# A two-layer convolution kernel on one core: every SBUF region that TensorE reads starts at one phase modulo 1024 bytes

## What is computed

```python
# layer 0: bottleneck with a deformable 3x3 convolution
out = relu(bn(conv1x1(x, w1)))                 # 1024 -> 256 channels
offset = conv3x3(out, w_off, b_off)            # 18 offsets per pixel
out = relu(bn(deform_conv3x3(out, offset, w2)))  # bilinear samples at 9 shifted places, 256 -> 256
x1 = relu(bn(conv1x1(out, w3)) + x)            # 256 -> 1024 channels
# layer 1: a kernel attention block
t, p, g = Wt @ x1, Wp @ x1, Wg @ x1            # 1024 -> 512 channels each
att[k] = sum(a_k * p**k * g);  y = sum_k a_k * att[k] * t**k    # k = 0, 1, 2, sums over a whole image
z = Wz @ y                                     # 512 -> 1024 channels
out = (z - mean) * rsqrt(var + eps) * gn_w + gn_b + x1          # mean, var over a whole image
```

## The kernel before

| tiles | stage, part in the matmul | before | after |
|---|---|---|---|
| `xh`, `xl`, `w1h`, `w1l`, `w2h`, `w2l` | 1, both operands | 544 (32) | 160 (32) |
| `o1h0`, `o1l0` / `o1h1`, `o1l1` | 1, both | 544 / 32 (32) | 160 / 672 (32) |
| `x1h`, `x1l` | 2, moving | 544 (32) | 160 (32) |
| `wlh0` to `wlh10`, `wll0` to `wll10`, `w3h`, `w3l` | 2, weights | 544 (32) | 160 (32) |
| `wlh11`, `wll11` | 2, weights of group 11 | 672 (32) | 160 (32) |
| `ao`, `acl`, `ident` | 2, transposes | 128, 544, 448 (0, 32, 64) | 160 (32) |
| `yh`, `yl`, `wzh` | 3, moving, weights | 544 (32) | 160 (32) |
| `wzl` | 3, weights of L196 | 128 (0) | 160 (32) |
| `g0_0` to `g1_2`, `xs`, `xb`, `tb` | not read by TensorE | 128 (0) | 160 (32) |
| `z44` to `z47`, `z70`, `stage`, `g1_3` | not read by TensorE | 672 (32) | 160 (32) |
| the other `z` tiles but `z69` | not read by TensorE | 544 (32) | 160 (32) |

## Time and profile before

### The profile page before, as it was taken

The page is one execution under the profiler, slowest core; times in us unless marked ns, Lnnn a source line. Parts: engine busy times, 40 slices in busy tenths (PEclk is TensorE's granted clock), DMA queues, the critical chain, the costliest instruction groups (busy, mean ns, idle before and its releaser), DMA issues.

```text
span 2339.6 us, 29804 instructions
## 1 busy us (share of the span) xinstructions
PE 2236.2 (96%) x10252; PEld 1853.8 (79%) x10252; DVE 1573.2 (67%) x3177; ACT 1252.9 (54%) x2432; POOL 794.7 (34%) x706
## 2 busy tenths in 40 slices
PE   8999999999989999999999999999999999999970
PEld 6888888888868888888888888888888878887750
DVE  4222324766788898889888988898884334467855
ACT  6444545453455565556555655565563324456745
POOL 0100003434224665566566766676651000000000
PEclk9999999999999999999999999999999999999985
DMA  9998889999998998898889889998883111118869
GB/s 304 313 314 287 303 299 376 399 401 393 403 374 290 315 333 312 305 327 315 304 308 326 307 305 312 318 322 307 310 319 128 72 54 36 54 52 295 313 229 388
DMA packets 289824, 667.97 MB, mean 286 GB/s; under 512 B 27112, under 2 KB 101608, under 8 KB 283528
## 3 DMA queue, kind: packets, MB, share of 16 engines
q0 software_dynamic: 88048, 322.81, 39.3%
q1 hardware_dynamic: 172536, 262.59, 31.5%
q10 hardware_dynamic: 29088, 80.67, 9.3%
HBM read 435.47 MB, written 230.49 MB: 285 GB/s over the span
## 4 chain that ended last, share of the span: by engine, by line
PE 87%; DVE 5%; DMA 4%; SPq 2%; ACT 1%; issue 1%; POOL 0%; ACTq 0%; DVEq 0%
PE bank L194 23%; PE bank L196 23%; PE bank L195 23%; PE bank L1458 5%; PE bank L1459 5%; PE bank L1460 5%; DVE z L1402 2%; PE bank L1476 2%; DMA xs<-x 1%; DMA g<-vwide,tbl 1%; SPq L458 1%; SPq L462 1%; PE bank L1500 0%; PE bank L1484 0%; DMA xt<-x 0%
## 5 line engine op out<-in xcount | busy, mean ns | idle before, releaser
L643 POOL DMA_INDIRECT g<-vwide,tbl x512 | 605.4, 1182 | 509.9 <-DVE a L1030 214.4
L194 PE MATMUL bank<-x1h,wlh 128*128 128x512 f32 x1536 | 603.1, 393 | 3.5 <-DVE x1l L1292 3.5
L196 PE MATMUL bank<-x1h,wll 128*128 128x512 f32 x1536 | 600.1, 391 | 0.0
L195 PE MATMUL bank<-x1l,wlh 128*128 128x512 f32 x1536 | 599.3, 390 | 0.0
L1030 DVE SCALAR_TENSOR_TENSOR a<-g,tbl,a 128x256 f32<-128x256 f32 x1224 | 529.0, 479 | 25.0 <-DMA g<-vwide,tbl 18.0
L670 ACT ACTIVATE g<-g,tbl 128x256 f32<-128x256 f32 x1008 | 427.1, 499 | 217.9 <-DMA g<-vwide,tbl 179.3
L194 PEld LDWEIGHTS bank<-x1h,wlh 128*128 128x128 f32 x1536 | 288.8, 188 | 64.0 <-issue 3.7
L196 PEld LDWEIGHTS bank<-x1h,wll 128*128 128x128 f32 x1536 | 288.6, 188 | 62.2
L195 PEld LDWEIGHTS bank<-x1l,wlh 128*128 128x128 f32 x1536 | 289.0, 188 | 60.7
L748 ACT ACTIVATE vb<-bank 128x512 f32<-128x512 f32 (+1 forms) x320 | 174.2, 554 | 191.1 <-PE bank L1460 161.4
L1458 PE MATMUL bank<-w2h,o1h 128*128 128x512 f32 (+1 forms) x640 | 236.7, 370 | 0.0
(11 more groups left out here) (154 smaller groups left out, 3206.6 us busy)
## 6 DMA issues: line engine op xcount, KB each, us to landing
vwide<-vb SPq DMA_DIRECT2D x256, 256.0 KB, 5.8
vwide<-vb SPq DMA_DIRECT2D x112, 512.0 KB, 5.3
xf<-in_x SPq DMA_DIRECT2D x32, 1024.0 KB, 6.4
x<-xf ACTq DMA_DIRECT2D x32, 1024.0 KB, 7.0
out<-z SPq DMA_DIRECT2D x128, 256.0 KB, 5.1
xin<-in_x ACTq DMA_DIRECT2D x54, 512.0 KB, 5.5
t<-ts ACTq DMA_DIRECT2D x64, 256.0 KB, 5.0
tb<-t POOLq DMA_DIRECT2D x16, 1024.0 KB, 5.8
```

The source lines that it names most:

```text
L194: nc.tensor.matmul(out, wh, xh, start=first, stop=False)
L195: nc.tensor.matmul(out, wh, xl, start=False, stop=False)
L196: return nc.tensor.matmul(out, wl, xh, start=False, stop=last)
L643: pool.indirect_dma_start(slot[:].rearrange("p a c -> p (a c)"), None, d["vwide"][img], bass.IndirectOffsetOnAxis(ap=at[:, i, tap(u), 0:1] ...
```

## The change

The memory map is shifted so that all blocks begin at one phase. The counter starts at 8352 instead of 8320; R1 is pushed up to the next address with the phase of G_AT; the `+ 128` in front of the last weights and the stage buffers goes; `ident` and `ones` stand before the tables `tbl`; the sums and coefficients of the attention (`gsum`, `sums`, `tot`, `coef`) move behind everything else. No instruction, wait, DMA or shape differs: on every engine and queue the instructions stand in the same order as before, with the same waits, and only their addresses are others.

```diff
     def __init__(self, nc):
         self.nc = nc
-        self.at = 8320
+        self.at = 8352
...
-    def region(self, size):
+    def region(self, size, phase=None):
+
+        if phase is not None:
+            self.at += (phase - self.at) % 1024
         at = self.at
         self.at += size
         return at
...
-    TBL = [m.put(f"tbl{i}", [128, 2, TAPS, 6]) for i in range(3)]
     IDENT = m.put("ident", [128, 128])
     ONES = m.put("ones", [128, 128])
+    TBL = [m.put(f"tbl{i}", [128, 2, TAPS, 6]) for i in range(3)]
...
-    GSUM = [m.put(f"gsum{i}", [128, CHUNKS * KCP]) for i in range(IMGS)]
-    SUMS = [m.put(f"sums{i}", [128, 2, KCP]) for i in range(IMGS)]
-    TOT, COEF = [m.put(f"tot{i}", [128, 3]) for i in range(IMGS)], [m.put(f"coef{i}", [128, 3]) for i in range(IMGS)]
...
-    R1 = m.region(16 * KB)
+    PHASE = G_AT % KB
+    R1 = m.region(16 * KB, PHASE)
...
+    assert R1 % KB == R2 % KB == PHASE
...
-    wl_at = [R2 + 16 * KB, R2 + 24 * KB] + [R3 + 8 * KB * i for i in range(6)] + [R5 + 40 * KB, R5 + 48 * KB, None, R5 + 60 * KB + 128]
+    wl_at = [R2 + 16 * KB, R2 + 24 * KB] + [R3 + 8 * KB * i for i in range(6)] + [R5 + 40 * KB, R5 + 48 * KB, None, R5 + 60 * KB]
...
-    STAGE_AT = [R5 + 68 * KB + 128, R5 + 60 * KB + 128, R5 + 64 * KB + 128]
+    STAGE_AT = [R5 + 68 * KB, R5 + 60 * KB, R5 + 64 * KB]
...
+    assert m.at <= R5 + 60 * KB
+    m.at = R5 + 72 * KB
+    GSUM = [m.put(f"gsum{i}", [128, CHUNKS * KCP]) for i in range(IMGS)]
+    SUMS = [m.put(f"sums{i}", [128, 2, KCP]) for i in range(IMGS)]
+    TOT, COEF = [m.put(f"tot{i}", [128, 3]) for i in range(IMGS)], [m.put(f"coef{i}", [128, 3]) for i in range(IMGS)]
```

## The result

The changed kernel takes 2352.6 us (median of 20 runs, 2340.22 to 2371.45), the kernel before 2361.06 us (20 runs, 2354.93 to 2382.98). The ratio is 0.9962, 95% interval 0.9944 to 0.9980: 9 us faster, by 4.7 to 13.2 us. The forecast was 2348.6 us, its range 2344 to 2356. The prediction gave 0.49 to a change of under 0.5% and 0.44 to a larger gain; the measured 0.4% is of the first kind.

A forecast was written before the change was run, and what follows sets the result against it. TensorE's own pace was taken to bound the kernel, PE being busy 96% of the span. Savings of 4.1 + 0.6 + 6.9 = 11.6 us took 2360.2 to 2348.6 us, range 2344 to 2356.

The forecast's parts named there:

- the price of mixed phases: On PE, matmuls in stretches whose operands start at mixed phases were claimed to cost 5 to 6 ns more each.
- Step 1: Projections: group 11's weights moved to the common phase save 4.1 us, and group 0 behind them 0.6 us.
- Step 2: Z product: wzl moved to the common phase saves 6.9 us: 5.1 in chunks 0 to 8, 1.1 in 14 and 15, 0.7 between.
- Step 3: Transposes: ident, ao and acl come to one phase; taken as nothing, bounds nothing and 1.4 us.
- Steps 4, 5 and 6: Convolution operands (with x1, o2, w3) moving together, DMA ends in SBUF, and ACT's and DVE's operands: nothing from each.
- The estimate of 6%: Final pass: by the skill page, a 2048-byte row costs 69 beats from 160 past a 256-byte multiple, 65 from 32 past.
- The rule on separate read ports: TensorE: weight load and moving operand read SBUF through separate ports, so phases would not matter and the time would stay.
- The sum against the median: Whole kernel: 11.6 us saved, taken from the median of 2360.2 us, with its 20.6 us above the profiled span left unchanged.
- no effect: Rival: the slow steps in groups 10 and 11 and z have another cause and stay, 2360 us; chance 0.10.
- slower: Rival: the phase itself costs and 160 is bad, so 6912 matmuls slow to 232.60 ns, 41 us, 2401 us; chance 0.07.
- stores slower: Rival: reading z from 160 costs the final pass's stores 6%, 2.8 us, giving 2351.4 us; chance 0.03.

The follow-up runs named there:

- the pair with small loads: The kernel before and the changed kernel, each with gathers from each buffer's second use replaced by loads of 64 bytes per partition: 2328.31 and 2319.80 us.
- the second profile of before: The kernel before, unchanged, profiled once more: time 2361.87 us, span 2360.1 us.
- the later set: The kernel before and the changed kernel, both unchanged, timed again side by side on another chip: 2355.7 and 2342.7 us, ratio 0.9950.

## Why the prediction was right

- *What bounds the kernel, and the price of mixed phases.* Right. 5.4 ns in groups 10 and 11 and 5.9 in z went away, each with its own edit. Phase modulo 1024 was more than is needed: agreement modulo 256 is enough.
- *Step 1, the weights of group 11 and the first half of group 0.* Forecast 4.7 us. Measured 0.30 us for a chunk without stalls (77.43 to 77.13), and 4.7 us over the stage in the pair with small loads. Right.
- *Step 2, wzl.* Chunks 0 to 8: forecast 5.1 us, measured 5.0. Chunks 9 to 15: forecast 1.1 + 0.7 = 1.8 us of 4.0. This stretch varies from run to run: 160.0 to 162.7 us in the five profiles with slow steps, 158.8 to 161.3 in five at the floor, means 160.9 and 159.6. That is 1.4 us, with an uncertainty of about 0.7 by the spread in each five. Chunks 14 and 15 gave their 1.1, so of the 2.85 us that chunks 9 to 13 could give most was lost, as forecast. That the waits for xs took it was argued from the waits of the profile before; no run took the xs loads away.
- *Step 3, transposes.* Taken as nothing. The changed kernel's groups 0, 1 and 4 still have their slow steps around the transposes. Right.
- *Steps 4, 5 and 6.* Groups 2 to 9 stayed at 43.52 us, the final pass at 75.6 against 75.2 us. Right. In the stores' stretch from 2319 to 2331 us a packet of 2048 bytes took 84 ns in both profiles (2374 of 2379 packets before, where most z tiles start 32 past a multiple of 256, and all 2379 after, where they start 160 past one). The estimate of 6% that the prediction works out from the Trainium skill (DMA: Bandwidth & Descriptors, How a descriptor splits into AXI transactions) is not borne out by that. The rule on separate read ports that it cites from the Trainium skill (TensorE: Matmul & The Clock Gate, Step-by-step: what each phase is for) does not hold as it was used there: by it the addresses would be of no account, and between the kernels with steps of 226.7 and of 233.3 ns nothing but addresses differs. What in the chip makes the two operands meet is not shown.
- *The sum against the median.* The step that failed is the sentence that the median lies 20.6 us above the span and that this stays as it is. A time lies only 1.8 us above its span. The other 19 us are, by the second profile of before (22.1 us of stalls in 2361.87 us), stalls in the projections that the first profile happened not to have. They are a term that the prediction did not know and that is as large as the gain. Without stalls the kernel before takes 2341.4 us by its first profile, and the changed kernel by an estimate from its own 2341.8 - 13.5 = 2328.3. So the medians hold some 19.7 and 24.3 us of stalls in the 20 runs each, and 14.3 and 14.4 in the later set. That the forecast's range held is partly luck: a term that varies by 10 us and more from run to run moved the difference by only a few us. What is shown is a gain in the stretches of 4.7 + 5.0 + 1.4 = 11.1 us, against 11.6 forecast; the intervals 4.7 to 13.2 us and (from 0.9950) 7.8 to 15.8 us both hold it. A change in the stalls of a few us either way is not excluded. In the pair with small loads, which has none, the medians still differ by only 8.5 us, less than the 9.7 us that the projections and z chunks 0 to 8 gave in its profiles; what took back the rest I cannot say from one profile of each.

The rival *no effect* fell by the steps, *slower* by the phases 128, 160 and 544 running alike, *stores slower* by the final pass. What in the gathers stops PE in the middle of a product is open. It was not tried to separate the rows' size, their scattered addresses and POOL's making of the descriptors.

## What to carry to other kernels

Put all tiles that TensorE reads at addresses that agree modulo 256 bytes, weights against the moving operand; which phase it is did not matter in the three that were tried for all tiles. One weight tile in three that disagrees slows the whole stretch. Read PE's pace from distances between starts in stretches without waits, since a mean duration of 391 against 395 ns hides what a step of 226.7 against 232.6 shows. Before a profile's span is set against a median, look whether the profiled execution is an ordinary one, and sum the stretches that differ.

## What was not expected of the hardware

- With weights 32, 128, 192 or 224 bytes before the moving operand, modulo 256, a matmul of 512 float32 columns takes 5.5 to 6.7 ns longer than the floor of 226.7; 64 before costs 2.2 ns, 64 behind 6.6, and 0, 256 and 512 nothing.
- The slow steps go on for eight or nine matmuls after the cause is gone, and one differing weight tile in three (160 modulo 256) costs 5.9 ns on the mean of all steps.
- While gathers run, PE stalls in the middle of products by up to 1.6 us at a time (in the kernel with only group 11 turned back), 0 to 33 us in all from run to run. One of the chips (medians of the kernel before 2339.3, 2355.7 and 2361.06 us in three sets of runs) was nearly free of it.
- Behind such a stall the granted clock can be at 1.2 GHz, for 3.4 or 6.8 us in the second profile of before, and each step takes 0.43 us in place of 0.23.
